# Softmax maxima of the last cross-attention as pairs of 64-row tiles, from the leading parts alone

## What is computed

```python
x_ = layernorm(ctx); lat = layernorm(x)                  # 77 and 512 rows
q = lat @ Wq + bq                                        # 16 heads of 64
k, v = split(concat([x_, lat]) @ Wkv + bkv)
sim = einsum('bhid,bhjd->bhij', q * 64**-0.5, k)         # 512 queries x 589 keys
sim = sim - stop_gradient(max(sim, -1))
out = softmax(sim) @ v                                   # then Wout, residual, layernorm
```

## Time and profile before

| | |
|---|---|
| median of 3 runs | 1247.82 us (1247.13 to 1249.44) |
| span of the profiled execution, first to last instruction | 1246.1 us |
| TensorE busy | 1139.7 us, 91% of the span |
| weight loads busy | 956.8 us, 77% |
| VectorE busy | 767.0 us, 62% |
| ScalarE busy | 601.9 us, 48% |
| GpSimd busy | 159.1 us, 13% |

### The profile page before, as it was taken

The page is one execution under the profiler, slowest core; times in us unless marked ns, Lnnn a source line. Parts: engine busy times, 40 slices in busy tenths (PEclk is TensorE's granted clock), DMA queues, the critical chain, the costliest instruction groups (busy, mean ns, idle before and its releaser), DMA issues.

```text
span 1246.1 us, 18545 instructions
## 1 busy us (share of the span) xinstructions
PE 1139.7 (91%) x7050; PEld 956.8 (77%) x7050; DVE 767.0 (62%) x1794; ACT 601.9 (48%) x1096; POOL 159.1 (13%) x117
## 2 busy tenths in 40 slices
PE   7749999989999856799999999999999999999896
PEld 4537888978888744688888988889888889889632
DVE  5774556475565677657666567665867656664247
ACT  4213232433333444556565556564656565664353
POOL 6130000120733614200000000000000000000001
PEclk9878878789999976799999999999999999999998
DMA  6000000000000100000000000000000000000001
GB/s 211 0 1 1 1 1 1 1 1 1 1 1 1 34 0 1 1 2 1 1 2 1 1 2 1 1 2 1 1 1 1 2 1 1 2 1 1 1 0 34
DMA packets 10550, 9.97 MB, mean 8 GB/s; under 512 B 3627, under 2 KB 9695, under 8 KB 9951
## 3 DMA queue, kind: packets, MB, share of 16 engines
q1 hardware_dynamic: 10463, 8.79, 2.2%
HBM read 7.60 MB, written 1.05 MB: 7 GB/s over the span
## 4 chain that ended last, share of the span: by engine, by line
PE 71%; ACT 14%; DVE 9%; issue 5%; POOL 0%; DMA 0%; POOLq 0%; DVEq 0%; ACTq 0%
PE PS L1368 66%; ACT KA L814 8%; ACT BIG L831 4%; PE PS L1380 4%; DVE X_ODD L882 1%; PE PS L1730 1%; DVE st L871 1%; DVE REG L904 1%; DVE X_EVEN L882 1%; DVE mv L874 0%; DVE mxm L1253 0%; ACT BIG L639 0%; DVE Y L918 0%; DVE Y L882 0%; DVE VXA L1220 0%
## 5 line engine op out<-in xcount | busy, mean ns | idle before, releaser
L1368 PEld LDWEIGHTS PS<-VXA,BIG 128*128 128x128 f32 (+1 forms) x3136 | 397.0, 192 | 47.6 <-ACT BIG L831 23.7
L1368 PE MATMUL PS<-VXA,BIG 128*128 128x65 f32 (+2 forms) x3136 | 399.3, 272 | 9.2 <-ACT BIG L831 9.2
L831 ACT ACTIVATE BIG<-PS 128x512 f32<-128x512 f32 (+1 forms) x320 | 187.0, 594 | 178.7 <-PE PS L1368 175.8
L1253 DVE TENSOR_REDUCE mxm<-PS 128x1 f32<-128x512 f32 x256 | 170.7, 688 | 98.3 <-PE PS L1368 94.0
L814 ACT ACTIVATE KA<-PS,b1s 64x512 fp32r<-64x512 f32 (+1 forms) x256 | 128.5, 502 | 51.5 <-PE PS L1368 45.8
L1368 PE MATMUL PS<-QA,KA 128*128 128x512 f32 (+1 forms) x320 | 145.7, 455 | 0.0
L510 POOL TENSOR_TENSOR rs<-ve,half_neg 128x4 f32<-128x4 f32 (+1 forms) x29 | 30.3, 1047 | 888.2 <-DVE ve L876 888.2
L1368 PE MATMUL PS<-QB,KB 128*128 128x512 f32 (+1 forms) x320 | 126.2, 394 | 0.0
L1368 PE MATMUL PS<-KA,QA 128*128 128x512 f32 (+1 forms) x512 | 116.2, 331 | 2.8 <-DVE mxm L1253 2.6
L1368 PEld LDWEIGHTS PS<-KA,QA 128*128 128x128 f32 x512 | 87.0, 190 | 23.0 <-DVE mxm L1253 4.8
L736 ACT ACTIVATE BIG<-PS 128x512 f32<-128x512 f32 x72 | 42.3, 596 | 96.6 <-PE PS L1368 96.3
(11 more groups left out here) (250 smaller groups left out, 1683.8 us busy)
## 6 DMA issues: line engine op xcount, KB each, us to landing
X_EVEN<-in_x SPq DMA_DIRECT2D x4, 256.0 KB, 3.8
VXA<-in_L_ffn_Wg SPq DMA_DIRECT2D x1, 1024.0 KB, 5.7
VXA<-in_L_ffn_Wu SPq DMA_DIRECT2D x1, 1024.0 KB, 7.8
VXA<-in_L_ffn_Wd SPq DMA_DIRECT2D x1, 1024.0 KB, 9.4
REG<-in_L_xattn_Wkv SPq DMA_DIRECT2D x1, 1024.0 KB, 4.9
QB<-crow SPq DMA_DIRECT2D x64, 2.0 KB
out<-X_EVEN SPq DMA_DIRECT2D x4, 256.0 KB, 2.3
wq1s<-in_L_xattn_Wq SPq DMA_DIRECT2D x1, 512.0 KB, 8.6
```

The lines of the kernel that those rows point to most:

```text
L831: act.activation(PX[0:rows, g % 4, :], PS[0:rows, g % 2, :], ACT.Exp, scale=SCALE_W).then_inc(pw_ready, 1)
L1253: dve.tensor_reduce(mxm[:, p % 2, h, m:m + 1], PS[:, 2 + g % 2, :], AX.X, ALU.max).then_inc(mu_free, 1)
L1368: return pe.matmul(dst, lhsT, rhs, start=start, stop=stop, **kw)
```

## The change

`MAX_UNITS` and `PROLOGUE` have five units in a step in place of ten: unit m of both heads at once, in slots 0, 1, 2, 3 (512 columns each) and 5 (the context columns). A unit writes head 0's scores into bank 2 and head 1's into bank 3. Each matmul takes only the 64 rows that hold the head's leading parts, at rows 0 to 63 for head 0 and 64 to 127 for head 1, and the two heads' matmuls are issued one behind the other. The number of matmuls and of columns is the same as before: per step 8 of 512 and 8 of 78. A unit waits until both reductions of the unit before are done, and VectorE waits for both matmuls before it starts its two reductions. The last combination of maxima is one instruction for both heads in place of two.

```diff
-MAX_UNITS = {0: [0], 1: [1, 2], 2: [3, 4], 3: [5, 6], 4: [7], 5: [8, 9]}
+MAX_UNITS = {0: [0], 1: [1], 2: [2], 3: [3], 5: [4]}
...
-             ("max", 0), ("max", 1), ("norm", 3), ("V", 0, 2), ("max", 2), ("max", 3), ("norm", 4), ("V", 0, 3), ("max", 4),
-             ("max", 5), ("norm", 5), ("latT", 2), ("V", 0, 4), ("max", 6), ("max", 7), ("V", 0, 5), ("max", 8),
-             ("max", 9), ("c", 0), ("Q", 1), ("V", 0, 6), ("K", 1), ("latT", 3), ("V", 0, 7), ("Kt", 1), ("V", 0, 8), ("V", 0, 9)])
+             ("max", 0), ("norm", 3), ("V", 0, 2), ("max", 1), ("norm", 4), ("V", 0, 3), ("max", 2),
+             ("norm", 5), ("latT", 2), ("V", 0, 4), ("max", 3), ("V", 0, 5), ("max", 4),
+             ("c", 0), ("Q", 1), ("V", 0, 6), ("K", 1), ("latT", 3), ("V", 0, 7), ("Kt", 1), ("V", 0, 8), ("V", 0, 9)])
...
-            def maxima(p, u):
-
-                h, m = divmod(u, 5)
-                g = 10 * p + u
-                dve.wait_ge(mu_full, g + 1)
-                if m < NT:
-                    dve.tensor_reduce(mxm[:, p % 2, h, m:m + 1], PS[:, 2 + g % 2, :], AX.X, ALU.max).then_inc(mu_free, 1)
-                else:
-                    dve.tensor_reduce(mxt[:, p % 2, h, :], PS[:, 2 + g % 2, 0:NT * (KEYS_PAD - S)].rearrange("p (t k) -> p t k", t=NT),
-                                      AX.X, ALU.max).then_inc(mu_free, 1)
-                    dve.wait_ge(mu_free, g + 1)
-                    dve.tensor_tensor(cmx[:, p % 2, h, :], mxm[:, p % 2, h, :], mxt[:, p % 2, h, :], ALU.max).then_inc(cm_ready, 1)
+            def maxima(p, m):
+
+                g = (NT + 1) * p + m
+                dve.wait_ge(mu_full, 2 * (g + 1))
+                for h in range(2):
+                    if m < NT:
+                        dve.tensor_reduce(mxm[:, p % 2, h, m:m + 1], PS[:, 2 + h, :], AX.X, ALU.max).then_inc(mu_free, 1)
+                    else:
+                        dve.tensor_reduce(mxt[:, p % 2, h, :], PS[:, 2 + h, 0:NT * (KEYS_PAD - S)].rearrange("p (t k) -> p t k", t=NT),
+                                          AX.X, ALU.max).then_inc(mu_free, 1)
+                if m == NT:
+                    dve.wait_ge(mu_free, 2 * (g + 1))
+                    dve.tensor_tensor(cmx[:, p % 2], mxm[:, p % 2], mxt[:, p % 2], ALU.max).then_inc(cm_ready, 1)
...
-            def max_unit(p, u):
-                h, m = divmod(u, 5)
-                g, r = 10 * p + u, p % 3
-                if u == 0:
+            def max_unit(p, m):
+
+                g, r = (NT + 1) * p + m, p % 3
+                if m == 0:
                     pe.wait_ge(hi_ready, 12 * (p + 1))
                     pe.wait_ge(pj_free, PJ["Kt", p] + 1)
-                if g >= 2:
-                    pe.wait_ge(mu_free, g - 1)
-                if m < NT:
-                    mm(PS[:, 2 + g % 2, :], QA[r][h][:, P * m:P * m + P], KA[r][h][:, 0:S]).then_inc(mu_full, 1)
-                else:
-                    w = KEYS_PAD - S
-                    for t in range(NT):
-                        ins = mm(PS[:, 2 + g % 2, w * t:w * t + w], QA[r][h][:, P * t:P * t + P], KA[r][h][:, S:KEYS_PAD])
-                    ins.then_inc(mu_full, 1)
+                if g:
+                    pe.wait_ge(mu_free, 2 * g)
+                w = KEYS_PAD - S
+                spans = [(m, 0, S)] if m < NT else [(t, w * t, w) for t in range(NT)]
+                for t, at, n in spans:
+                    for h in range(2):
+                        rows = slice(DW * h, DW * h + DW)
+                        keys = slice(0, S) if m < NT else slice(S, KEYS_PAD)
+                        ins = mm(PS[:, 2 + h, at:at + n], QA[r][h][rows, P * t:P * t + P], KA[r][h][rows, keys])
+                        if t == spans[-1][0]:
+                            ins.then_inc(mu_full, 1)
...
-                    pe.wait_ge(cm_ready, 2 * (p + 1))
+                    pe.wait_ge(cm_ready, p + 1)
```

More of the change, by code:

```diff
@@ L1679, in pv @@
                 ins.then_inc(pv_ready, 1)
-            def max_unit(p, u):
-                h, m = divmod(u, 5)
-                g, r = 10 * p + u, p % 3
-                if u == 0:
+            def max_unit(p, m):
+                g, r = (NT + 1) * p + m, p % 3
+                if m == 0:
                     pe.wait_ge(hi_ready, 12 * (p + 1))
-                    pe.wait_ge(pj_free, PJ["Kt", p] + 1)
-                if g >= 2:
-                    pe.wait_ge(mu_free, g - 1)
-                if m < NT:
-                    mm(PS[:, 2 + g % 2, :], QA[r][h][:, P * m:P * m + P], KA[r][h][:, 0:S]).then_inc(mu_full, 1)
-                else:
-                    w = KEYS_PAD - S
-                    for t in range(NT):
-                        ins = mm(PS[:, 2 + g % 2, w * t:w * t + w], QA[r][h][:, P * t:P * t + P], KA[r][h][:, S:KEYS_PAD])
-                    ins.then_inc(mu_full, 1)
+                if g:
[9 more added lines that the diff above has]
+                            ins.then_inc(mu_full, 1)
             def task(key):
```

## The result

The changed kernel takes 1271.45 us (median of 4 runs, 1267.25 to 1273.46) against 1247.63 for the kernel before on the same chip: ratio 1.0176, 95% interval 1.0152 to 1.0201: 22 us slower by the ratio, 24 by the medians. (The ratios in this document are not quotients of two medians and differ from them by up to 0.2%.) The forecast was 1238.0, faster, with a range from 1234 to 1266; both the direction and the range were missed.

A forecast was written before the change was run, and what follows sets the result against it. TensorE was taken as the loop's bound. Steps with V work save 0.57 us, those without 0.12, together -10.5 us from 1246.1: span 1235.6, median 1237.3, rounded to 1238.0; range 1234 to 1266.

The forecast's parts named there:

- u: TensorE time one new pair unit adds in its slot; taken as 0.25 us, bounded by 0.235 and 0.775.
- the nearest row, `c`: Transpose between `pv` and scores, a 128 x 32 tile; its 0.05 us was taken to show that switching tiling is free.
- The upper bound: Most a tiling switch could cost: 0.16 us matmul tail plus 0.11 bare weight load, 0.27 each way.
- sign for the drain: Timeline gap of 0.1 us or more ahead of the first 64-row load, or of the `pv` behind the unit.
- half a drain: Pair units at 0.5 us with some VectorE waits left: +14 us, near 1262; chance 0.10.
- rival 3: Tiling switches drain TensorE around each pair unit, 0.775 us a unit, VectorE waits vanish: +45 us, 1293; chance 0.12.
- 4u - 1.84: Per-step change in slots 0 to 3 without waits: four new units less the old units' 1.84 us.
- rival 2: A unit's two matmuls run one behind the other, 0.47 us a unit: +14 us, 1262; chance 0.16.
- rival 1: Second head's weights load only once the first matmul starts, 0.34 us a unit: no change, 1247; chance 0.20.
- The waits of the hand-over: TensorE waiting for both VectorE reductions: 0.27 us in unit 2 every step, 0.45 more in unit 3 without V work.
- Slots 4 and 5: Behind K, ScalarE's chain sets the time; the unit there is free up to 1.22 us and gains nothing.
- the hole: TensorE's 0.31 us wait for ScalarE's exponential ahead of slot 7's `pv`, once a step; gains in slots 4 and 5 only widen it.

The follow-up runs named there:

- probec32: Kernel before plus one unread 8-column matmul ahead of each `pv`, over all 128 rows but 32 columns of weights: ratio 1.0152.
- probe64: Kernel before plus one unread 8-column matmul ahead of each `pv`, over rows 0 to 63 only: ratio 1.1028.
- probe128: Kernel before plus one unread 8-column matmul ahead of each `pv`, over the whole 128 x 128 array: ratio 1.022.
- same_rows: Changed kernel, but units 0 to 3 take two pieces of one head, so both matmuls use the same half of the array: 1304.7 us, ratio 1.0452.
- pair128: Changed kernel's five pair units and order, but each maxima matmul over all 128 rows: 1264.12 us, ratio 1.0133 to the kernel before.

## Why the prediction was wrong

**The step that failed is the cost of a pair unit**, and in it the price of switching the array's tiling. I had bounds of u = 0.235 and 0.775 and took 0.25, "the lower end", because "the nearest row, `c`, says that the switch is free". The row was read rightly: `c` costs 0.05 us, and `probec32` confirms that a change of columns is free. But it was the wrong neighbour. A change of rows costs 0.40 us there and back for a tile with hardly any work (`probe64`), of which 0.11 is what any extra load costs (`probe128`). Of the 0.635 us of a unit, 0.235 are streaming. The rest is 0.10 of tail and a bare load of 0.10 on each side. That the 0.10 is the tail of the matmul in flight is a reading: its place and size are in the rows, and no run tells it from another wait of this length. The upper bound (0.16 of tail and 0.11 of load each way) was near: only its tail was too long, by 0.06. The prediction's own sign for the drain, a gap ahead of the first 64-row load, is what the row shows.

**The rule that I set aside holds for rows.** The Trainium skill (TensorEngine Tiling (Array Packing), Key Properties) says that a change of the tiling mode drains the TensorE; by the rows above that holds for rows, and did not show for columns. I had weighed it at 0.12 for the full and 0.10 for half a drain. The measured case lies between the two. Its price, by the same sum as for rival 3, would have been 1269; the median is 1271.

**The other terms held.** The units' 1.84 us before and the rule that a step's loss is 4u - 1.84 where the waits vanish: +0.70 worked out, +0.68 measured. The overlap of the two heads, which rival 2 denied, is there (`same_rows`), and rival 1's lag of loads isn't: the loads overlap as well. The waits of the hand-over stand in `pair128` with the price that the prediction gave them (+14 us, +14.6 from `c` to `c`), and vanish behind the drain, as rival 3 said, if only just in slot 3. The 0.27 us in every step and 0.45 in those without V work that my sum had for them were therefore no part of the changed kernel's time; at u = 0.25 they would have been, but no run has such a unit. Slots 4 and 5 counted for nothing: the unit there takes 0.33 + 0.57 + 0.91 - 0.235 - 0.81 = 0.77 us, within its cover of 1.22. The 0.14 that it saved against the 0.91 of before brought nothing: the `pv` of slot 6 now starts 0.26 behind the second score matmul in place of 0.23 and its first load is bare (810.89, 1.11 long), and the hole is 0.33 in place of 0.31. The prologue gave 0.6 us, within what was allowed.

**The chances were wrong in shape.** A bound that is seen in no row should have kept more weight than one row of another kind of switch took from it. Both ends of u were known, and the break-even, u = 0.35, lay in the lower quarter between them.

## What to carry to other kernels

Before two half-height matmuls are packed side by side, count the changes of row tiling: on this chip each pair of changes cost 0.4 us, the streaming time of nearly two 512-column matmuls, while packing two such matmuls saves 0.235. By these numbers it can pay only if at least two such pairs run between two changes (2 x 0.235 against 0.40), which no run here tried. A row for the "same" kind of event is evidence only if it changes the same thing; a probe of 8 columns in each slot would have told rows from columns. And a dense engine's short hole is worth a look by itself: one unit moved into it gave 6.6 us, two thirds of the 10 that the forecast had for the whole packing with free changes, for an edit of the order alone.

## What was not expected of the hardware

- A change from 128 rows to 64 and back costs about 0.40 us around a matmul of 8 columns, its bare load with it; a change from 128 columns of weights to 32 and back costs 0.12, as much as the same matmul without a change (0.11).
- Two weight loads of 64 rows each, for the two halves, take 0.19 us together, as one alone; two matmuls of 512 columns take 0.51 in all.
- The label of the loads' idle time, mxm or "issue", changes from unit to unit while the gap stays at 0.36 us, also where the reductions had ended 2 us earlier: the engine named was not what the load waited for.
- The granted clock fell in stretches in which TensorE was busy nearly all the time: with all units behind `pv` to a mean of 0.86 in 550 to 600 us at 98% busy (down to 0.50, the 1.2 GHz level, in 746 to 750 us, at 100%), and in `probe64` to 0.57 in 670 to 690 us at 100%, with no wait at all. With the context unit back ahead of `pv` it stayed at the upper level from 600 to 1100 us. What brings it down is open.
